# A two-layer decoder whose steps change from 128 tokens of each of four sequences to 512 consecutive tokens of one

## The reference, cut to what matters

```python
# layer 0, attention: retention, 8 heads of 32; within a chunk and a state carried from chunk to chunk
attn = einsum('bhid,bhjd->bhij', qc, kc) * D
o = attn @ vc + (qc * decay_q) @ S
S = decay_s * S + (kc * decay_k).T @ vc
# layer 1, attention: linear attention, 64 wide; S is a running sum over the tokens of a sequence
kv_cumsum = cumsum(sigma_k outer v, axis=1);  k_cumsum = cumsum(sigma_k, axis=1)
local = (sigma_q @ kv_cumsum) / (sigma_q . k_cumsum);  combined = g * memory_output + (1 - g) * local
# both layers: cross-attention on 77 context rows of the same sequence, 16 heads of 16
x1 = layernorm(x + attention);  p = softmax(q k^T) over 77;  x2 = layernorm(x1 + (p v) W_out)
# both layers: a mixture of experts over all tokens
# layer 0: 64 experts of width 64, 8 for each token, and 2 shared experts of width 512 for all tokens
# layer 1: 8 gated experts of width 512, 2 for each token
x3 = layernorm(x2 + sum_k weight_k * expert_k(x2))
```

## Time and profile before

| | us |
|---|---|
| timed runs, median of 3 (lowest, highest) | 1877.52 (1873.45, 1879.04) |
| span of the profiled execution | 1981.9 |
| PE busy, share of that span | 1687.5, 85% |
| DVE busy | 1165.2, 59% |
| POOL busy | 892.7, 45% |
| ACT busy | 623.2, 31% |
| attention of layer 0 | 0 to about 600 |
| experts of layer 0 | about 600 to 1106 |
| attention of layer 1 | about 1106 to 1530 |
| gated experts of layer 1 | about 1530 to 1982 |

### The profile page before, as it was taken

The page is one execution under the profiler, slowest core; times in us unless marked ns, Lnnn a source line. Parts: engine busy times, 40 slices in busy tenths (PEclk is TensorE's granted clock), DMA queues, the critical chain, the costliest instruction groups (busy, mean ns, idle before and its releaser), DMA issues.

```text
span 1981.9 us, 45543 instructions
## 1 busy us (share of the span) xinstructions
PE 1687.5 (85%) x17739; PEld 1329.8 (67%) x17739; DVE 1165.2 (59%) x3228; ACT 623.2 (31%) x957; POOL 892.7 (45%) x1000
## 2 busy tenths in 40 slices
PE   6788888887689889998998478889977599999994
PEld 4566665666566567666676355667666499999994
DVE  4576655665432177776656456788765245655564
ACT  1232322222231277454555223445432111111110
POOL 0017556655758102888888856333323102222223
PEclk9999989998689999999998779999987699999997
DMA  9416543555448899888998922113111512333332
GB/s 325 150 46 199 184 150 116 190 169 191 146 147 237 219 304 295 285 278 273 297 294 290 317 78 82 57 65 121 69 39 65 164 49 76 91 94 98 98 94 69
DMA packets 269634, 322.61 MB, mean 163 GB/s; under 512 B 25083, under 2 KB 245487, under 8 KB 268655
## 3 DMA queue, kind: packets, MB, share of 16 engines
q1 hardware_dynamic: 234559, 226.38, 36.1%
q0 software_dynamic: 33024, 92.32, 14.4%
q10 hardware_dynamic: 1840, 1.00, 0.2%
HBM read 157.22 MB, written 162.40 MB: 161 GB/s over the span
## 4 chain that ended last, share of the span: by engine, by line
PE 68%; DVE 10%; issue 6%; DMA 6%; ACT 4%; POOL 3%; another core or an unknown queue 2%; SPq 1%; DVEq 1%; POOLq 0%; ACTq 0%
PE wide L2067 13%; PE d_yp L2079 6%; PE wide L110 4%; PE wide L127 4%; PE wide L1199 4%; PE wide L1202 3%; PE wide L1728 3%; PE e_yp L1739 3%; PE wide L1186 3%; PE bank L1033 3%; PE bank L1212 3%; PE bank L1219 2%; PE e_xp L1716 2%; PE bank L1105 2%
## 5 line engine op out<-in xcount | busy, mean ns | idle before, releaser
L1441 POOL DMA_INDIRECT big<-results,slots x256 | 263.4, 1029 | 202.1 <-DMA results<-e_y 125.5
L2067 PE MATMUL wide<-d_xt,d_ws 128*128 128x128 f32 x2272 | 279.0, 277 | 0.6 <-issue 0.6
L2067 PEld LDWEIGHTS wide<-d_xt,d_ws 128*128 128x128 f32 x2272 | 272.7, 193 | 4.5 <-issue 1.0
L597 POOL DMA_INDIRECT lists<-big,slots x160 | 159.6, 997 | 116.7 <-DVE slots L961 70.3
L663 ACT ACTIVATE pt<-wide 77x2048 f32<-77x2048 f32 x64 | 119.8, 1871 | 196.5 <-PE wide L1202 118.7
L1936 POOL DMA_INDIRECT d_picked<-results,slots x64 | 64.0, 1001 | 182.0 <-DMA results<-d_y 168.7
L1967 ACT ACTIVATE d_gate<-wide 128x512 f32<-128x512 f32 x71 | 42.4, 597 | 323.9 <-PE wide L2067 323.9
L2079 PE MATMUL d_yp<-d_wd,d_h 128*128 x568 | 134.2, 379 | 0.0
L1456 DVE SCALAR_TENSOR_TENSOR big<-big,weights 128x256 f32<-128x256 f32 x256 | 108.9, 487 | 41.6 <-DMA big<-results,slots 28.2
L110 PE MATMUL wide<-shared_sx,shared_sw 128*128 128x512 f32 x256 | 126.3, 616 | 7.7 <-DMA shared_sx<-res_t 5.2
L127 PEld LDWEIGHTS wide<-shared_sw,shared_sh 128*128 128x128 f32 x512 | 97.3, 191 | 45.1 <-issue 29.6
(11 more groups left out here) (280 smaller groups left out, 3488.8 us busy)
## 6 DMA issues: line engine op xcount, KB each, us to landing
lists<-zero SPq DMA_DIRECT2D x20, 2048.0 KB, 14.6
e_x<-lists SPq DMA_DIRECT2D x80, 512.0 KB
results<-e_y SPq DMA_DIRECT2D x80, 512.0 KB
d_x<-lists SPq DMA_DIRECT2D x71, 128.0 KB
results<-d_y SPq DMA_DIRECT2D x71, 128.0 KB
e_w<-in_L_w SPq DMA_DIRECT2D x2, 4096.0 KB
shared_sw<-in_x_t SPq DMA_DIRECT2D x32, 128.0 KB
x<-in_x SPq DMA_DIRECT2D x8, 512.0 KB
```

The lines of the kernel that those rows point to most:

```text
L597: pool.indirect_dma_start(out=lists, out_offset=bass.IndirectOffsetOnAxis(ap=slots[:, b, i, k:k + 1], axis=0), in_=z2[i % 3][:, b, :], in_ ...
L1441: pool.indirect_dma_start(out=picked[:, c % NG, b, :], out_offset=None, in_=results[0:-(-PAGES_OF_STEP[s] // 4) * 4 * R0, :], in_offset=ba ...
L2067: ins = mm(out[T % 2][:, a * P:(a + 1) * P], ws[:, T % NW, n, c, a * P:(a + 1) * P], xt[:, T % 2, c], start=c == 0, stop=c == KC - 1)
```

## The change

A step becomes 512 consecutive tokens of one sequence: block j of step s is tokens s*512 + j*128 on, counted through all sequences, and a sequence is two steps (`HALVES`). With it:

- `sc` and `pv` take all 512 tokens at once: part p is no longer a block but one of four (c, h), a half of the heads' columns and rows. A part of `sc` is 8 products of 512 columns, one of `pv` 4. DVE's share of `pv` divides one h at a time into `ratio` and transposes it back once for two parts. `att_done` counts two per step, and `wout` waits for both.
- the state goes from block to block within a step. Layer 0: DVE does four decayed additions one after the other, three of them ahead of the `state`, so `up` stands before `mix`, and `mix` waits for it. Layer 1: `up` makes eight (five in a sequence's second half) products into three sums, DVE does four operations in a row, `carry` takes the state on; `up` of the same step stands before `num`, which waits for all of it.
- in `mix` the state's part is one product of 128 columns by a 128-column stationary side, where there were four with 32.
- rows and columns of a step are contiguous in memory: the four DMAs of `load_t`, of the transposed rows out and of `load_rows` become one each.
- both lists are reordered: in layer 0 the last `pv` moves behind the next round's first `wo`, `b2` between the last `sc` and `pv`; `kt` and the key halves of `qk` come earlier.

The diff, cut to that:

```diff
+TS = NB * P
+STEPS = NT // TS
+HALVES = SEQ // TS
+def rows_of_step(dram, s):
+    return dram[s * TS:(s + 1) * TS].rearrange("(j p) n -> p j n", p=P)
     def load_rows(self, sp, src_t, s):
-        for b in range(NB):
-            at = b * SEQ + s * P
-            sp.dma_start(self.sx[:, s % 2, :, b * P:(b + 1) * P],
-                         src_t[:, at:at + P].rearrange("(c p) n -> p c n", p=P)).then_inc(self.sx_in[s % 2], 16)
+        sp.dma_start(self.sx[:, s % 2], src_t[:, s * TS:(s + 1) * TS].rearrange("(c p) n -> p c n", p=P))\
+            .then_inc(self.sx_in[s % 2], 16)
 SEQUENCE0 = [
...
+    ("wo", 1, 0), ("pv", 2, 3), ("wo", 1, 1), ("put", 3, 0), ("v", 0, 0), ("v", 0, 1), ("ln1", 1, 0),
+    ("wout", 2, 0), ("wout", 2, 1), ("cwt", 3, 0), ("put", 3, 1), ("qk", 0, 2), ("x1t", 1, 0), ("x1t", 1, 1),
+    ("mx", 1, 0), ("ln2", 2, 0), ("qk", 0, 3), ("mx", 1, 1), ("res", 1, 0), ("put", 3, 2),
+    ("kt", 0, 0), ("qk", 0, 0), ("x2t", 2, 0), ("x2t", 2, 1), ("mx", 1, 2), ("put", 3, 3), ("qk", 0, 1), ("mx", 1, 3),
+    ("put", 3, 4), ("kt", 0, 1), ("ret", 0, 0), ("put", 3, 5), ("up", 0, 0), ("mt", 1, 0), ("rt", 2, 0), ("put", 3, 6),
+    ("put", 3, 7), ("sc", 1, 0), ("mix", 0, 0), ("top", 2, 0), ("ret", 0, 1), ("pv", 1, 0), ("sc", 1, 1), ("mix", 0, 1),
+    ("rank", 2, 0), ("sc", 1, 2), ("pv", 1, 1), ("b2", 3, 0), ("sc", 1, 3), ("pv", 1, 2), ("b2", 3, 1),
 SEQUENCE1 = [
...
+    ("kvt", 1, 0), ("mt", 3, 0), ("wo", 2, 0), ("wo", 2, 1), ("up", 1, 0), ("sc", 3, 0), ("ln2", 4, 0), ("num", 1, 0),
+    ("num", 1, 1), ("rank", 5, 0), ("sc", 3, 1), ("x2t", 4, 0), ("ln1", 2, 0), ("x2t", 4, 1), ("pv", 3, 0), ("sc", 3, 2),
...
                 if stage == "up" and first:
+                    for j in range(NB - 1):
+                        decayed(j + 1, j, 0)
+                        step(decayed(j + 1, j, 1))
                     for g in range(2):
                         ins = nc.vector.tensor_tensor(
                             state[:, :, g], total[:, :, g].unsqueeze(2).broadcast_to([P, NB, 4, RD]),
                             state_mask[:, g].unsqueeze(1).broadcast_to([P, NB, 4, RD]), ALU.mult)
                     ins.then_inc(state_done, 1)
...
                 if stage == "up" and not first:
+                    nc.vector.tensor_copy(ahead_of[0:MEM], carry[0:MEM])
+                    step(nc.vector.tensor_tensor(ahead_of[MEM:P], carry[MEM:P], sums[MEM:P, 0], ALU.add))
+                    step(nc.vector.tensor_tensor(behind, ahead_of, sums[:, 1], ALU.add))
+                    if i % HALVES < HALVES - 1:
+                        empties(nc.vector.tensor_tensor(carry[:], behind, sums[:, 2], ALU.add), job)
...
                 if stage == "pv":
+                    by_head = turned[:].rearrange("p (t e) -> p t e", e=2 * XD)
+                    step(nc.vector.reciprocal(rden[:], by_head[:, :, XD]))
+                    step(nc.vector.tensor_tensor(
+                        ratio[:].rearrange("p (t h e) -> p t h e", h=2, e=XD)[:, :, h], by_head[:, :, 0:XD],
+                        rden[:].unsqueeze(2).broadcast_to([P, NB * P // 32, XD]), ALU.mult))
+                    if h:
+                        nc.vector.transpose(att_t[:, c], ratio[:]).then_inc(att_done, 1)
...
-                            for r in range(4):
-                                mm(out[quarter(r), at:at + P], state[:, b, g, r], qk[:, g, toks(b)], start=True,
-                                   stop=False, skip_group_check=True)
+                            mm(out[:, at:at + P], state[:, b, g].rearrange("p r n -> p (r n)"), qk[:, g, toks(b)],
+                               start=True, stop=False, skip_group_check=True)
...
                 if stage == "num":
-                    if i:
-                        emptied(pe, ("up", i - 1, 0))
-                    emptied(pe, ("kvt", i, 0))
+                    emptied(pe, ("up", i, 0))
...
                 if stage == "sc":
+                    c, h = p // 2, p % 2
+                    for r in range(4):
+                        mm(out[0:CTX, r], keys[quarter(r), i // HALVES, c, h * CTX:(h + 1) * CTX], qt[quarter(r), c],
+                           start=True, stop=False)
+                    for r in range(4):
+                        ins = mm(out[0:CTX, r], sel[quarter(r), p], peak_t[quarter(r)], start=False, stop=True)
...
                 if stage == "pv":
+                    for r in range(4):
+                        ins = mm(out[quarter(r)], vals[:, i // HALVES, c * 8 + 2 * r + h],
+                                 pt[0:CTX, p % 2, r * TS:(r + 1) * TS], start=True, stop=True)
...
-                    pe.wait_ge(att_done, NB * i + 2 * p + 2)
+                    pe.wait_ge(att_done, KC * (i + 1))
```

More of the change, by code:

```diff
@@ L303, in attention_phase @@
         late = sb("late", [P, NB, E])
[L304 to L305 removed]
+        turned = None if first else sb("turned", [P, TS])
+        ratio = sb("ratio", [P, TS])
         chosen = sb("chosen", [P, NB, E])
@@ L511, in _ @@
                     filled(sp, ("v", n, 1))
-                    filled(sp, ("qk", n, 3))
+                    for a in range(4):
+                        filled(sp, ("qk", n, a))
                     sp.dma_start(units.sw2[:], d["sw2"].rearrange("e (c p) n -> p (e c) n", p=P)).then_inc(units.sw2_in, 16)
-                    filled(sp, ("up", n, 0))
+                    filled(sp, ("mix", n, 1))
                     for e in range(ES):
@@ L1005, in _ @@
                     fills(ins, ("key", b, 0))
-            if first:
-                pe.wait_ge(state_done, 1)
-            else:
+            if not first:
                 pe.wait_ge(ready, READY)
```

145 lines of the change are left out of this document (59 added, 86 removed), and 13 rows, old and new, of tables (SEQUENCE0, SEQUENCE1).

## The result

The changed kernel takes 1926.69 us in the median of 4 runs (1925.16 to 1932.58); the kernel before took 1877.44 beside it (1873.45 to 1879.04). The ratio of the runs is 1.0294 with a 95% interval of 1.0261 to 1.0328: slower. The two medians alone differ by 49 us (1.0262); the ratio on record stands for 55 us, with 49 to 61 as its interval. The forecast was 1899, a loss of 21.5 us, with a range of 1825 to 1917, so the sign was right, the loss was more than twice as large as forecast, and the range did not hold it. The kernel before was timed again in each session of this study, and its median lay between 1870.9 and 1877.4 us. One ratio is uncertain by 0.2 to 0.4%.

A forecast was written before the change was run, and what follows sets the result against it. It took PE as the bound in the gated phase and nearly in layer 1, with layer 0's stalls mostly the profiler's. 22 - 17 + 10 + 16 + 3 - 4.5 - 8 = +21.5 us, from 1877.5 to 1899, range 1825 to 1917.

The forecast's parts named there:

- The stalls: Attention rounds of both layers: 90 us or more in the profile, mostly the profiler's own; a tenth real would give -8.
- sc and pv at 0: Attention products of both layers: four times wider and four times fewer take the same streaming time, 0, bounds -13 to +19.
- mix at +22: Layer 0's `mix`: changing between full-width and 32-column products costs 2.8 us a round, x 8 = +22 us.
- The waits for the exponential at -17: Layer 0: `b2` and `wo` fill PE's waits for ACT ahead of the last `sc` and `pv`, -2.1 x 8 = -17 us.
- up ahead of mix at +10: Layer 0: DVE reaches the router's maximum and second mask later, +1.2 x 8 = +10 us, between 0 and +25.
- num behind up at +16: Layer 1: `num` waits 2.0 us for DVE's sums every round, x 8 = +16; bounds 0 to +4 us a round.
- rival 4: Waits pull the clock down: 2 us more in each round of both layers, +30, 1929 us; chance 0.07.
- DMAs at -4.5: One DMA for four: 1.5 us sooner at the start, 3 us less wait for rows at 654.46, together -4.5.
- 1 (stalls are real): Stalls of both layers are in timed runs too, so some 80 of 90 us go: -50, 1827 us; chance 0.27.
- 2 (fewer instructions): Fewer products are worth about 10 ns each, -25 us: 1874, or 1837 by the page's 25 ns; chance 0.06.
- 3 (waits are filled): `num` doesn't wait and `mix` changes shape at half price: -5, 1872 to 1880 us; chance 0.15.
- 5 (wide products don't share the array): Wide products queue for the same rows, so `sc` doubles, +1.7 x 64 = +109: 1985 us; chance 0.02.

The follow-up runs named there:

- e5: The kernel before the change, unchanged, profiled once more: span 1867.9 us, timed median 1869.51 us, ratio 0.9988.
- e2: The changed kernel with `sc` and `pv` again in products of 128 columns, four times as many: 1926.43 us, ratio 1.0300.
- after: The changed kernel itself, with the whole change: 1926.69 us, ratio 1.0294.
- e15: The kernel before the change, with both parts of `wout` waiting for the results of all four `pv`: 1878.92 us, ratio 1.0034.
- before: The kernel without the change, timed again in each session: 1877.44 us beside the changed kernel.
- e9: The kernel before the change, with `pv(2,3)` behind the first `wo` and `b2` moved into the waits for the exponential in layer 0: 1871.19 us, ratio 0.9999.
- e10: As e9, and the second part of `v` moved between `pv(1,0)` and `sc(1,1)` in layer 0: 1852.65 us, ratio 0.9914.
- e13: As e10, but `b2` back in its old place between two parts of `mx`: 1850.92 us, ratio 0.9890.
- e8: The changed kernel with layer 0's `up` behind the second part of `mix`, so `mix` uses the previous step's states: 1915.31 us, ratio 1.0247.
- e12: As e11, and layer 0's `up` behind `mix` as in e8: 1885.40 us, ratio 1.0087.
- e11: The changed kernel with the state's product of `mix` in four quarters and layer 1's `up` between the parts of `wo`: 1892.62 us, ratio 1.0116.
- e3: The changed kernel with layer 1's `up` between the two parts of `wo` instead of behind both: 1907.25 us, ratio 1.0179.
- e4: The changed kernel with two unread 128x512 products ahead of `num` in layer 1, filling its wait: 1912.23 us, ratio 1.0201.
- e7: The kernel before the change, with layer 1's `up` behind the second `wo`, `num` waiting for it, and three more dependent DVE operations: 1901.97 us, ratio 1.0169.
- e14: The kernel before the change, with only the second part of `v` moved between `pv(1,0)` and `sc(1,1)`: 1857.18 us, ratio 0.9933.

## Why the prediction was wrong in size, point by point

**The stalls.** The reading that carried the sign was that timed runs have no such stalls as the earlier trace rows. That was right: e5 has the same kernel with rounds of 54.4 and a span of 1867.9 beside a timed median of 1869.51. The reason given for it was wrong. It is not a cost of the profiler that goes with small instruction records, since e2 has 17395 product records and none of it; it was one odd execution. The -8 us for residual stalls should have been 0. The forecast span of 1930 came near 1923 by luck, through two errors that cancel: a cost of the change of 29.5 where it was 55, and 81 us of stalls taken off where the span of the same kernel fell by 114.

**sc and pv at 0.** Right for the products: e2 and after differ by 0.06%. The two groups of a wide `sc` (from 1220.77 to the end of the second, 1.95 us) take what eight narrow ones do (1.99 us from 177.64 on in the kernel before, profiled again). But the step looked at the products alone and missed who waits: with `pv` by pairs of heads, `wout` can't start on half of them. Where a round goes on behind it, that is hidden; at the end of a layer it isn't. e15 prices it at +6 us. It was in neither the sum nor the rivals.

**mix at +22.** Mechanism and size in the round were right: 0.75 us for a block and group against the forecast 0.79, and no gain for PE. On the clock it was worth 17 in after and 9 in before, two numbers that their uncertainties don't separate. The step that was too coarse is the last, "x 8": PE's time was taken for the round's, although half of it falls into waits that were there anyway, for the second mask in before and for the exponential in after.

**The waits for the exponential at -17.** This is the step that failed: 0 in e9. The two waits are gone, as forecast, but the term took what PE no longer waits for as the gain of all eight rounds. The jobs that fill the waits were not free where they came from. `b2` had filled PE in the last rounds of layer 0, where there are no `qk` products to stand between the parts of `mx`; e10 and e13 differ in its place alone, and the last stretch is 98.0 us with it moved and 91.6 without. And the gain of 2.05 us a round came in full (2.2 and 1.9) only where the clock stayed full behind the mask, and as 0.4 where it fell. The seven rounds together gave 10.5 us in the profile, and the last stretch took 9.0 of them back. Why the clock fell there, and not behind the same waits of the kernel before, stays open.

**up ahead of mix at +10.** 9 us by e8, 5 by e12 against e11, neither of them clear of noise. The rounds of e8 are 8.8 us shorter in the profile. Nothing speaks against the term.

**num behind up at +16.** The wait was right (2.0 us forecast, 2.02 in the row above). The term was mis-sized: it is 21 us by e3, which leaves 0.65 us of the wait in place, 17 by e4, which keeps the dependency and fills the time, and 32 by e7 in the kernel before; with the 3 us for `up` the forecast had 19. What was missing is the low clock behind the wait, 1.6 us for the pair of `sc` and up to 1.4 more for the small products ahead of it, in four of six full rounds. The prediction had it twice, as the upper bound of this term ("up to 4 us a round, if the idle time pulls the clock down") and as rival 4 with 1929 us, and gave it 7 in 100. Yet the earlier trace rows, on which the prediction leant for the stall, show just this: products at half speed behind a pause. The row was at hand, and it should have moved the value, not only the bound.

**DMAs at -4.5.** Of the 1.5 us at the start most is there: the first product comes at 8.1 to 9.0 us in the profiles of the changed kernel and its variants, and at 9.3 to 10.4 in those of the kernel before. The other 3 are not. PE's idle time ahead of the shared experts' first products, with what ended most of it, in before and after:

```profile
L110 PE MATMUL wide<-shared_sx,shared_sw 128*128 128x512 f32 x256 | 129.7, 631 | 5.4 <-DMA shared_sx<-res_t 2.9
```

```profile
L115 PE MATMUL wide<-shared_sx,shared_sw 128*128 128x512 f32 x256 | 127.2, 620 | 6.0 <-DMA shared_sx<-res_t 3.6
```

The 13.8 us of the earlier trace rows belonged for the most part to the stray execution.

**The sum.** Measured one by one: mix 17, up 9, num and layer 1's `up` 21 (e3, not all of it), wout 6, filled waits 0, DMAs -1, which is 52 of the 55 us of the ratio. The agreement is better than the numbers deserve: most of them are uncertain by 8 us or more, and with the first three undone together (e12) 16 us are left, of which `wout` explains 6. So about 10 us, most of them in layer 1, have no cause shown. Three gains of the forecast were not there: 17 for the filled waits, 8 for the stalls, 3 of the 4.5 for the DMAs. Without them it would have been 21.5 + 28 = +49.5. Against that mix came 5 lower and up 1, num 2 higher at least, and wout's 6 were missing. The largest single error is the term for the filled waits: the forecast counted -17 where e9 gives 0.

**The rivals.** 1 (stalls are real) is refuted by e5. 2 (fewer instructions) is refuted by e2. The Trainium skill, "TensorEngine Tiling (Array Packing)", section "Instruction Overhead", states some 60 cycles of overhead for each matmul. If they added to products that follow each other, the 2304 products more of e2 would cost 58 us by the prediction's 25 ns each, an estimate from that page; measured are 1 us, uncertain by 9. 3 (waits are filled) is refuted by the rows of `num`. 4 (waits pull the clock down) was at work in layer 1, and in some rounds of layer 0, but not in each round, as it was priced. 5 (wide products don't share the array) is refuted by the 1.95 us of `sc`; its own sum was off as well, since 1899 and 109 make 2008 and not 1985.

## What to carry to other kernels

A wait of 2 us of PE can have two prices: the wait, and the products behind it at the low clock. The second was about as large as the first in layer 1 here, and in other rounds, behind waits just as long, it was nothing; it has to be read from the rows behind the wait. Filler work whose result nobody needs gives back the second; a job moved up into the gap can give back both. A job is only free to move if the place it leaves had no use for it, and the rounds at the end of a pipeline, which have fewer jobs, must be looked at on their own. And before stalls of a profile are explained, the kernel should be profiled a second time: a single profiled execution that is more than 5% off the timed ones may be a stray, and its phases are then no base for a sum.

## What the runs showed of the hardware that was not expected

- Products that nobody reads made the kernel faster: 16 of them (1.9 us a round) gave 17 us (e4), since the two groups behind them took 1.10 and 1.03 us instead of 2.01 and 1.75.
- Of waits of PE of 2.1 to 2.7 us, some had low clock behind them and some had not, in one and the same place of the list: in layer 0 of the kernel before the clock stayed full behind five of six, in the changed kernel behind two of six. What decides it wasn't found.
- 4608 more product records, with `sc` and `pv` in products of a quarter of the width, made no difference that could be measured: 1926.43 against 1926.69 us.
- One profiled execution of the kernel before had a span of 1981.9 us, another 1867.9, with trickles of small products in the first alone. The cause of the trickles wasn't found.
- Moving a single job of 1.73 us to a later place in the same round gave 12.5 us of 1871 (e14), with 1.0 to 1.9 us in six of the seven rounds.
